# Attention scores on TensorE: stationary tiles of 64 rows and 128 keys instead of four square tiles of 64 by 64

## What is computed

```python
B, N, S, DIM, HEADS, DHEAD = 16, 64, 1024, 256, 16, 64
lat = layer_norm(latents, ln_lat_g, ln_lat_b)
ctx = layer_norm(context, ln_ctx_g, ln_ctx_b)
q = (lat @ Wq).reshape(b, n, HEADS, DHEAD).transpose(0, 2, 1, 3)
k, v = jnp.split(ctx @ Wkv, 2, axis=-1)          # each to (b, heads, s, dhead)
k = apply_rope(k, cos[None, None], sin[None, None])
attn = jnp.einsum('bhnd,bhsd->bhns', q, k) * DHEAD ** (-0.5)
attn = jax.nn.softmax(jnp.clip(attn, -11.0, 11.0), axis=-1)
out = jnp.einsum('bhns,bhsd->bhnd', attn, v)     # then @ Wo + bo, and the rest of the layer
```

## Time and profile before

| | us |
|---|---|
| median of 3 runs | 1230.54 |
| lowest, highest | 1227.43, 1234.68 |
| the profiled execution | 1237.52 |
| its span, first to last instruction | 1235.8 |
| main loop of the cross attention, in the span | about 55 to 947 |
| linear attention and start of the experts | 947 to 1083 |
| experts | 1083 to 1236 |

### The profile page before, as it was taken

The page is one execution under the profiler, slowest core; times in us unless marked ns, Lnnn a source line. Parts: engine busy times, 40 slices in busy tenths (PEclk is TensorE's granted clock), DMA queues, the critical chain, the costliest instruction groups (busy, mean ns, idle before and its releaser), DMA issues.

```text
span 1235.8 us, 39825 instructions
## 1 busy us (share of the span) xinstructions
PE 1183.8 (96%) x16268; PEld 998.4 (81%) x16268; DVE 1021.3 (83%) x1954; ACT 650.5 (53%) x1089; POOL 609.2 (49%) x611
## 2 busy tenths in 40 slices
PE   7999999999999999999999999999999999899997
PEld 3778788878778788778877878778888788789997
DVE  6799889989888899889988988889767366668886
ACT  7556555554545555545554545555444233356674
POOL 2466556555655555556555655556443133333332
PEclk8999999999999999999999999999999999999999
DMA  6366565556555566555656656565653530566662
GB/s 231 80 165 155 147 149 137 143 139 170 144 135 150 138 154 158 142 134 134 151 143 153 149 134 147 138 148 142 167 114 100 188 127 31 190 205 174 204 197 64
DMA packets 136173, 181.36 MB, mean 147 GB/s; under 512 B 30316, under 2 KB 96312, under 8 KB 135864
## 3 DMA queue, kind: packets, MB, share of 16 engines
q1 hardware_dynamic: 110552, 150.80, 45.8%
q10 hardware_dynamic: 21360, 23.80, 7.6%
q0 software_dynamic: 4080, 4.22, 1.7%
HBM read 81.93 MB, written 30.56 MB: 91 GB/s over the span
## 4 chain that ended last, share of the span: by engine, by line
PE 87%; DVE 4%; issue 3%; DMA 2%; ACT 2%; SPq 1%; POOL 1%; POOLq 0%; ACTq 0%; DVEq 0%
PE bank L1579 29%; PE bank L1608 27%; PE bank L1565 10%; PE bank L1934 6%; PE bank L1631 3%; PE bank L1738 2%; PE bank L1984 2%; PE bank L1985 2%; PE bank L1986 1%; PE bank L1791 1%; PE bank L1815 1%; PE bank L1834 1%; DMA x_slots<-xn_all,slot 1%; DMA w_two<-in_L_ffn_W_dram 1%; PE bank L1824 1%
## 5 line engine op out<-in xcount | busy, mean ns | idle before, releaser
L1579 PE MATMUL bank<-ct,wk_hi 128*128 128x512 f32 x1024 | 328.6, 402 | 5.3 <-DVE kr_third L1119 3.1
L1608 PE MATMUL bank<-p_hi,xc 128*128 128x512 f32 x1024 | 316.1, 390 | 0.0
L1579 PEld LDWEIGHTS bank<-ct,wk_hi 128*128 128x128 f32 x1024 | 189.7, 190 | 46.3 <-DVE kr_third L1119 3.7
L1118 DVE TENSOR_TENSOR kw<-bank,stab 128x512 f32<-128x512 f32 x256 | 175.7, 686 | 62.0 <-PE bank L1579 56.1
L1608 PEld LDWEIGHTS bank<-p_hi,xc 128*128 128x128 f32 x1024 | 192.1, 188 | 39.9
L593 POOL TENSOR_TENSOR kr<-kr,ksw 128x1024 f32<-128x1024 f32 x64 | 154.4, 2412 | 106.8 <-issue 104.0
L1579 PE MATMUL bank<-ct,wk_lo 128*128 128x512 f32 x512 | 202.2, 395 | 0.0
L1608 PE MATMUL bank<-p_lo,xc 128*128 128x512 f32 x512 | 199.3, 389 | 0.0
L783 ACT CAST p_hi<-pr 128x1024 fp32r<-128x1024 f32 x128 | 134.4, 1050 | 95.2 <-DVE pr L1086 95.2
L1106 DVE TENSOR_TENSOR p_lo<-pr,p_hi 128x1024 fp32r<-128x1024 f32 x128 | 169.0, 1321 | 0.5 <-ACT p_hi L783 0.4
L778 ACT ACTIVATE pr<-bank 128x1024 f32<-128x1024 f32 x128 | 126.8, 1026 | 61.1 <-PE bank L1565 61.1
(11 more groups left out here) (227 smaller groups left out, 2023.5 us busy)
## 6 DMA issues: line engine op xcount, KB each, us to landing
ksw<-kw SPq DMA_DIRECT2D x512, 128.0 KB, 2.3
x_turned<-xt SPq DMA_DIRECT2D x120, 128.0 KB
ct_read<-x_turned SPq DMA_DIRECT2D x30, 512.0 KB
w_two<-in_L_ffn_W_dram SPq DMA_DIRECT2D x15, 1024.0 KB, 5.0
raw<-in_ctx_dram ACTq DMA_DIRECT2D x56, 256.0 KB, 3.9
x_slots<-fill ACTq DMA_DIRECT2D x32, 258.0 KB, 3.7
w_all<-in_L_ffn_W_dram SPq DMA_DIRECT2D x4, 2048.0 KB, 17.2
wo<-in_L_ffn_W_dram SPq DMA_DIRECT2D x7, 1024.0 KB, 5.2
```

What stands on the lines that cost most here:

```text
L1118: dve.tensor_tensor(by_tile(kw[:, i, cols]), keys_, by_tile(stab[:, places]), ALU.mult).then_inc(kw_done, 1)
L1579: last = pe.matmul(psK[:, a * 512:(a + 1) * 512], l[:, k, w], ct[:, h % 3, r, k], start=(m == 0), stop=(m == len(parts) - 1))
L1608: last = pe.matmul(psZ[c], xc[:, slot_, l, t, cols], r[:, i, :, t], start=(f == 0 and m == 0), stop=(f == 1 and m == len(parts) - 1), skip ...
```

## The change

The loop over the two halves `c` of a context tile's keys goes. One matmul now has all 128 keys of the tile as its stationary columns and writes all 128 partitions of the bank. The two heads remain side by side, each in 64 rows of the array, so two matmuls at a time cover the array in place of four. What is computed, the operands read, the banks written and every wait are the same; a step has 16 matmuls in the code in place of 32.

```diff
                     for t in range(HT):
                         for a, g in enumerate(pairs_of(j)):
-                            for c in range(2):
-                                cols = slice(a * 512 + t * P + c * N, a * 512 + t * P + (c + 1) * N)
-                                for h in range(2):
-                                    rows = slice(h * DH, (h + 1) * DH)
-                                    last = pe.matmul(banks[c * N:(c + 1) * N, h, t * 2 + a], kr_at(j)[rows, cols], qo[rows, g, at:at + N],
-                                                     start=True, stop=True)
+                            cols = slice(a * 512 + t * P, a * 512 + (t + 1) * P)
+                            for h in range(2):
+                                rows = slice(h * DH, (h + 1) * DH)
+                                last = pe.matmul(banks[:, h, t * 2 + a], kr_at(j)[rows, cols], qo[rows, g, at:at + N], start=True, stop=True)
                     last.then_inc(s_ps, 1)
```

## The result

| | before | after |
|---|---|---|
| median, us (4 runs each) | 1230.93 | 1310.18 |
| lowest to highest | 1227.43 to 1234.68 | 1308.39 to 1312.21 |
| the profiled execution | 1237.52 | 1308.39 |
| its span | 1235.8 | 1306.6 |

The ratio is 1.0644, with a 95% interval of 1.0608 to 1.0679: 79 us slower. The forecast was 1320, with a range of 1290 to 1352.

The account below looks back on a forecast made before the run. TensorE, busy 864.4 of 892 us in the main loop, was taken to bound the kernel. On the profiled 1237.5 us, dearer scores add 113 and vanished gaps return 27: 1324; with the lower median, 1320 us, range 1290 to 1352.

Parts of the forecast that it names:

- What bounds the kernel: Main loop: TensorE, busy 864.4 of 892 us, sets the time, so its added work counts in full, but for the gaps.
- The price of a group: Scores: a group of two wide tiles costs 0.112 us, a pair of steps 3.78 in place of 2.02, 113 us in all.
- The reading of L1867 and L1791: Matmuls with 128 stationary columns start 0.117 and 0.111 us apart moving 8 or 128 columns, so the load sets the distance.
- L1815: Nearest row, four tiles of 32 rows by 128 columns: they load side by side at one load's price, 0.112 to 0.118 us.
- rival 1: Scores: groups cost what they do today, a pair 2.02 us; 1210 us, or no change if gaps stay; chance 0.07.
- What comes back: Scores: 15 gaps, likely from fetching instructions, cost 26.6 us and all go; minus 27, bounds 0 and minus 27.
- keys and sums keep their duration: Sign for the profile after: TensorE's keys and sums in the main loop last as long as before, no change.
- the sum: Whole kernel: the profiled 1237.5 plus 113 for the scores minus 27 for the gaps makes 1324 us.
- The two base times: Whole kernel: from the profiled 1237.5 us 1324, from the median 7.0 us lower 1317 or 1324; 1320 was said.
- Cover: Main loop: VectorE and GpSimd get more room and stay covered; if VectorE delayed TensorE 0.2 us a pair, 13 us.

Follow-up runs that it names:

- a_move32: The changed kernel, but from step 2 on each matmul of the scores moves only 32 of the 64 latents; 1355.11 us.
- a_move128: The changed kernel, but half of the scores' matmuls move 128 latents in place of 64, with the same results; 1308.95 us.
- a_turns: The changed kernel with the two heads one after the other in each step, same matmuls and results; 1686.03 us.
- b_cols32: The kernel before, from step 2 without each pair's second head, the first head's scores in four tiles of 64 rows by 32 columns; 1238.94 us.
- b_split_due: The kernel before, with keys of step j + 4 between the scores of j and j + 1 only in pairs with outputs ahead; 1228.14 us.
- b_onehead: The kernel before, but from step 2 on the scores of each pair's second head are left out; 1200.95 us.

## Why the prediction was right

**What bounds the kernel** held: TensorE was busy from 55 to 1018 us without a break afterwards, and the loss on it came through in full.

**The price of a group** was right, and for the reason given. It was 3.72 us a pair for 3.78 forecast; per pair +1.70, so 64 pairs cost 109 us for the 113 forecast. The reading of L1867 and L1791, that the load of the stationary columns sets the distance, is shown by a_move32 and a_move128 (no change from 32 to 128 moving columns). That row tiles load side by side, taken from L1815, is shown by a_turns. The Trainium skill has the rule as well (TensorE: Matmul & The Clock Gate, "LDWEIGHTS (loading the stationary operand)"): a load takes the number of its columns over 1.2 ns. By it, 64 and 128 columns would take 53 and 107 ns, an estimate; the distances here are 58 and 112. The rule that I weighed as rival 1, a pack that costs one matmul whatever is loaded, has failed: it would have left the pair at 2.02.

**What comes back** was right in its cause and too small in size. The prediction counted 26.6 us, all at the scores, and these did come back (155.5 - 64 x 2.01 = 26.9). It missed what hangs on them, and had "keys and sums keep their duration" among its signs. After three of the gaps the clock fell. The table by stretch of the kernel before shows it around one of them (the number ahead of the last two is the clock):

```profile
336.00:340.30 4.30, 2.15 (x136) 2.00 (x127) 2.21 (x6) 1.40 (x2) 3.51 (x3) 1.00 0.44 88
340.30:344.90 4.60, 4.60 (x21) 3.60 (x14) 1.29 (x2) 4.34 (x7) 0.73 (x1) 0.63 0.30 108
```

and so does its chain, in order of time (start, us, piece):

```profile
336.10 1.61 PE bank L1565 x107
337.71 2.15 issue
339.86 0.57 PE bank L1565 x21
340.42 4.54 PE bank L1579 x12
```

The twelve keys behind the gap took 4.54 us in place of 2.95, at a granted clock of 0.63. Three times this is 4.8 us. The clock fell a fourth time in the main loop, behind a wait of 2.7 us for VectorE at 91 us: 1.7 us at the keys behind it. One more gap stood in the keys behind the scores, 1.8 us with what followed, and a short one 0.4: together 8.7 of the 9.1 us by which the keys became cheaper. Of the wait for VectorE 0.4 us is left, and that is nearly all of the 3.0 us by which the sums, where it stood, became cheaper; why it shrank no run tests. The piece of 4.54 us was in the chain, which I had read only for its shares.

**What the sum missed on the other side** is a small one: the outputs, square tiles, are now followed by another tiling, and take 1.09 us in place of 0.98 from their first matmul to the scores, 3.3 us in all.

**The two base times.** Against the profiled executions the forecast was 1324 and the result 1308.4: 4 us from the pair, 12 from keys and sums, 3 from the experts (chance, see above), less 3 for the outputs. Against the medians it was 1320 for 1310.2. The profiled execution of before was 6.6 us above the median of its runs and that of after 1.8 below. The kernel before varies more, from 1227 to 1237 in all runs; that this is the gaps' doing is likely, but no run settles it.

**Cover.** That the other engines would have more room held: VectorE was busy for 788.9 us of the 892 before and for 710.2 after.

## What to carry to other kernels

By these runs a group of small float32 matmuls side by side costs the longer of its stationary load and its moving stream, so widen the stationary tile only where the moving side is at least as long: here 64 stationary to 64 moving columns was the balance, and with 128 to 64 the load, twice as long, set the price. Read that from a row that moves almost nothing and one that moves much with the same stationary size. And look at how many instructions TensorE gets in a few microseconds: a gap in the middle of a burst that nothing releases may be code that hasn't arrived (count the instructions from one such gap to the next), and taking it away must cost less than it does, in tiling changes and in an engine with little slack.

## What the runs showed of the hardware

- The granted clock falls not only behind idle time. With 32 moving columns and 128 stationary ones (a_move32) TensorE was busy all along, and the keys behind the scores ran slow in 23 of 64 pairs, in the stretch shown at a clock of 0.55; with 64 columns (after) it stayed at 1.00 from 55 to 947 us. With one tile at a time (a_turns) the mean was 0.82 from 55 to 1400 us, again without idle time. That cost 45 us and an estimated 200.
- In the kernel before, the three longest gaps (2.0 to 2.15 us) were each followed by keys at a low clock (0.63 over 4.6 us around one); the 12 of 0.8 to 1.8 us were not. The length of the gap alone doesn't decide: in b_cols32 keys ran slow behind eight gaps, at the scores, of 1.0 to 1.9 us and not behind one of 1.7.
- In the kernel before, a block of 256 TensorE instructions run through in 1.83 to 1.97 us was followed by a gap of 0.8 to 2.2 us in 16 of 16 cases; one in 2.01 us was not, and behind the 87 slower ones no gap was longer than 0.25 us. In b_cols32 it was 16 of 17 blocks of 1.91 to 1.99 us. Two gaps came behind slower blocks, which stays unexplained: 1.8 us behind one of 4.1 in b_split_due, and 0.6 us behind one of 2.8 in b_onehead.
- A further change between tilings cost about 0.4 us, 0.16 at the scores, 0.09 at the keys and 0.14 at the sums; what it consists of inside TensorE no run shows.
